# Roll layer of a fused two-block model: unread products gathered ahead of a step's first turns, the projection's bias moved to VectorE, and another split of the 32 images into groups

## The reference, cut to what matters

```python
h = h + _L1_attn_ref(_layernorm(h), W_A, W_V, W_O, b_O)
h = h + _L1_ffn_ref(_layernorm(h), ...)

def _L1_attn_ref(x, W_A, W_V, W_O, b_O):
    z = softmax(einsum('bse,he->bsh', x, W_A) * SCALING, axis=1)
    roll = z^T[:, :, (i - j) % S] * tril
    v = einsum('bse,fe->bsf', x, W_V)
    out = einsum('bhij,bjhd->bihd', roll, v)
    return einsum('bse,fe->bsf', out, W_O) + b_O
```

## Time and profile before

| | |
|---|---|
| median of 3 runs | 1064.62 us (1059.83 to 1065.32) |
| profiled execution | 1058.96 us, its span 1057.2 us |
| TensorE busy | 950.0 us (90%) |
| VectorE busy | 582.8 us (55%) |
| GpSimd busy | 519.2 us (49%) |
| ScalarE busy | 413.2 us (39%) |
| roll layer, first turn to last routing logits | 656.1 to 861.3 us of the span |

### The profile page before, as it was taken

The page is one execution under the profiler, slowest core; times in us unless marked ns, Lnnn a source line. Parts: engine busy times, 40 slices in busy tenths (PEclk is TensorE's granted clock), DMA queues, the critical chain, the costliest instruction groups (busy, mean ns, idle before and its releaser), DMA issues. The chain is left out here.

```text
span 1057.2 us, 29755 instructions
## 1 busy us (share of the span) xinstructions
PE 950.0 (90%) x10428; PEld 746.9 (71%) x10459; DVE 582.8 (55%) x1446; ACT 413.2 (39%) x1102; POOL 519.2 (49%) x714
## 2 busy tenths in 40 slices
PE   8899999998747999999999997689999957999996
PEld 6667777777634888888888875355556635888895
DVE  1778888865994777433333325677886452111111
ACT  2267677734243343343443422223333222332431
POOL 0055665620604777777777627777772002333432
PEclk9999999999969999999999998899999987999998
DMA  7010000002004988877788723334455047476750
GB/s 257 1 46 2 0 0 0 2 11 75 1 1 156 307 276 260 273 245 223 243 265 254 229 89 100 105 112 124 125 140 220 22 159 251 142 255 230 266 156 25
DMA packets 79821, 149.30 MB, mean 141 GB/s; under 512 B 18892, under 2 KB 53327, under 8 KB 75760
## 3 DMA queue, kind: packets, MB, share of 16 engines
q1 hardware_dynamic: 34768, 77.15, 21.5%
q0 software_dynamic: 17712, 47.88, 15.7%
q10 hardware_dynamic: 27248, 23.09, 6.5%
HBM read 200.22 MB, written 31.73 MB: 219 GB/s over the span
## 5 line engine op out<-in xcount | busy, mean ns | idle before, releaser
L1332 POOL DMA_INDIRECT x_x<-m_x_rows,x_idx x170 | 165.7, 975 | 74.7 <-issue 36.1
L1358 PE MATMUL x_pup<-x_xt,x_w 128*128 128x128 f32 (+1 forms) x2176 | 182.9, 250 | 0.0
L1358 PEld LDWEIGHTS x_pup<-x_xt,x_w 128*128 128x128 f32 (+1 forms) x2176 | 166.9, 165 | 5.9 <-issue 5.7
L1623 POOL DMA_INDIRECT rl_y<-m_y_rows,rl_idx x136 | 132.7, 976 | 43.6 <-issue 38.1
L1439 DVE TENSOR_TENSOR x_hid<-x_gate,x_pup 128x128 f32<-128x128 f32 x170 | 48.9, 287 | 147.9 <-ACT x_gate L1411 141.1
L1372 PE MATMUL x_pdown<-x_w,x_hid 128*128 128x256 f32 (+1 forms) x408 | 104.2, 389 | 0.2 <-DVE x_y L1446 0.2
L1407 ACT ACTIVATE x_xt<-x_pturn 128x256 f32<-128x256 f32 x170 | 65.2, 383 | 89.1 <-PE x_pturn L1343 86.4
L442 POOL TENSOR_TENSOR wa_probs<-wa_probs,wa_peak 68x544 f32<-68x544 f32 x64 | 69.9, 1092 | 57.6 <-DVE wa_peak L593 54.9
L2405 DVE TENSOR_TENSOR x_y<-x_pdown,x_b 128x256 f32<-128x256 f32 x21 | 8.9, 424 | 149.2 <-PE x_pdown L2359 149.2
L2391 ACT ACTIVATE x_hid<-x_pup,x_b 128x128 f32<-128x128 f32 (+1 forms) x200 | 52.6, 356 | 93.1 <-PE x_pup L2342 92.9
L1411 ACT ACTIVATE x_gate<-x_pup 128x128 f32<-128x128 f32 x170 | 47.1, 277 | 92.5 <-PE x_pup L1358 91.8
(11 more groups left out here) (345 smaller groups left out, 1917.9 us busy)
## 6 DMA issues: line engine op xcount, KB each, us to landing
x_w<-in_experts SPq DMA_DIRECT2D x204, 384.0 KB
late_w<-in_w SPq DMA_DIRECT2D x28, 1024.0 KB, 12.5
m_y_rows<-x_y ACTq DMA_DIRECT2D x170, 128.0 KB
xT<-in_w SPq DMA_DIRECT2D x12, 1024.0 KB, 7.0
xn<-in_w SPq DMA_DIRECT2D x10, 1024.0 KB, 11.5
h<-in_w SPq DMA_DIRECT2D x10, 1024.0 KB, 15.3
m_x_rows<-xn SPq DMA_DIRECT2D x34, 128.0 KB, 1.9
x_x<-m_x_rows,x_idx POOLq DMA_INDIRECT x170
```

Of the source, the lines that this page charges most:

```text
L1332: nc.gpsimd.indirect_dma_start(x[:, s, :], None, x_rows, bass.IndirectOffsetOnAxis(ap=idx[:, s:s + 1], axis=0))\
L1358: mm = nc.tensor.matmul(pup[rows:rows + wide, bank, m * P + side * wide:m * P + (side + 1) * wide], w[:, lane, first:first + wide], xt[:, ...
L1623: nc.gpsimd.indirect_dma_start(y[:, t % YR, kk, :], None, y_rows, bass.IndirectOffsetOnAxis(ap=idx[:, n:n + 1], axis=0))\
```

## The change

Four edits in `roll_layer`:

- Sizes: `[2] + [4] * 6 + [2] * 3`. There are now 10 groups and 13 steps; what was a group of 4 and one of 2 images at the end is now three groups of 2.
- Unread products: in steps where `1 < g1 < NG - 1` none stands between the parts any more, nor the wait that went with each. Six stand ahead of the first turn (three where the group has two images). In steps 1 and 2 there are 20 ahead of the first turn beside the old ones, in the last such step 4. After the last group the row of 8 is 5.
- Bias: `project` has no product with `b_o`. VectorE adds `b_o` to `h` with one instruction a tile, once the tile has been normalised.
- Loads of the guessed weights: ahead of group 4's stores. It was group 5 (`NG - 4` with `NG` = 9).

```diff
-    SIZES = [2] + [4] * 7 + [2]
+    SIZES = [2] + [4] * 6 + [2] * 3
...
-                    if g == NG - 4:
+                    if g == 4:
...
                     for s, t in enumerate(tiles_out(g)):
-                        nc.tensor.matmul(pr[:, s, :], ident, late["b_o"][:, :], start=True, stop=False)
                         for c in range(DC):
                             mm = nc.tensor.matmul(pr[:, s, :], aT[:, c, t * P:(t + 1) * P], late["w_o"][:, c, :],
-                                                  start=False, stop=(c == DC - 1))
+                                                  start=(c == 0), stop=(c == DC - 1))
                     mm.then_inc(projected, 1)
+
+                def steady(g):
+                    return 1 < g < NG - 1
...
                 def fill_values(g, n):
+                    if steady(g):
+                        return
                     pe.wait_ge(v_moved, pairs_through(g))
...
                 def fill_mid(g, n):
+                    if steady(g):
+                        return
...
+                    if has1:
+                        fill(g1, 6 * SIZES[g1] // GI if steady(g1) else 20 if g1 < 2 else 4)
                     for t in tiles_in(g1):
                         turn("in", t)
-                        fill(g1, 1)
+                        if not steady(g1):
+                            fill(g1, 1)
                     if has1:
-                        fill(g1, 1)
                         mix_logits(g1)
...
                     if has2 and not has1:
-                        fill(g2 + 1, 8)
+                        fill(g2 + 1, 5)
...
+                def add_out_bias(ts):
+                    for t in ts:
+                        dve.wait_ge(normed, turn_at["in", t] + 1)
+                        nc.vector.tensor_tensor(h[:, t, :], h[:, t, :], late["b_o"][:, :], ALU.add).then_inc(out_biased, 1)
+
                 def add_projected(g):
                     ts = tiles_out(g)
                     dve.wait_ge(projected, g + 1)
+                    dve.wait_ge(out_biased, ts[-1] + 1)
...
                     if outs:
                         scale("out", outs)
+                    add_out_bias(tiles_in(g1))
```

More of the change, by code:

```diff
@@ L1573, in roll_layer @@
         plog = po[:, GC:GC + NT * E1]
-        (indexed, set_up, added, in_measured, out_measured, logged, rooted, scaled, normed, turned, turn_moved, z_done, z_moved,
+        (indexed, set_up, added, out_biased, in_measured, out_measured, logged, rooted, scaled, normed, turned, turn_moved, z_done, z_moved,
          z_shifted, exped, z_normed, z_turned, zt_moved, zf_done, zf_moved, v_done, v_moved, forwarded, terms,
          inverted, out_moved, projected, proj_added, logits, rows_out, chain) = sems(
-            nc, k, "rl", "indexed set_up added in_measured out_measured logged rooted scaled normed turned turn_moved z_done "
+            nc, k, "rl", "indexed set_up added out_biased in_measured out_measured logged rooted scaled normed turned turn_moved z_done "
             "z_moved z_shifted exped z_normed z_turned zt_moved zf_done zf_moved v_done v_moved forwarded terms "
```

## The result

| | before | after |
|---|---|---|
| median | 1062.61 us (7 runs, 1058.72 to 1066.2) | 1072.28 us (7 runs, 1070.06 to 1081.79) |
| ratio, 95% interval | | 1.012 (1.0089 to 1.0151) |
| profiled execution | 1058.96 us, span 1057.2 | 1078.26 us, span 1076.5 |
| TensorE busy | 950.0 us (90%) | 959.8 us (89%) |
| VectorE busy | 582.8 us | 591.0 us |

The kernel became slower: by 9.7 us (0.9%) in the medians, and by 1.2% in the ratio over all runs, since the seven runs of after are spread upward. A gain was forecast. Its base was 1064.6 us, the median of three runs; seven runs put before at 1062.61.

The account below looks back on a forecast made before the run. TensorE bounds at 22.19 us a step, fetches close at 20.5. Last logits 7.6 us earlier (853.7), less 0.6 for the clock: gain 7.0, so 1064.6 becomes 1057.6 us; range 1052.5 to 1064.0.

Parts of the forecast that it names:

- Rival 3: TensorE idles some 3 us a step without products between parts, so the clock falls; 12 falls give 1072 us; chance 0.08.
- TensorE's step: Steps of 4 images: 2.91 us gained less 1.28 lost, so 20.56 us instead of 22.19, near the fetches' pace.
- Bias: VectorE's additions ahead of the combinations: 0.41 us each, 0.83 a step, covered by its wait for ScalarE.
- First steps: Turns at 656.1 to 696.40: fetches set them, and 20 products (4.3 us) fit into idle, nothing gained or lost.
- Loads: Moved to group 4, they delay tile 13's fetches by 3.3 us (0 to 7.4); its turn comes 2.4 us late.
- Clock behind that wait: Low clock behind the wait at 781 us, taken as half of 1.27 us: 0.6 us lost.
- Tail of small groups: From that turn to the last logits: 72.3 us instead of 76.3, 4.0 us less despite one step more.
- What follows keeps its length: Routing and experts behind the last logits take 196 us as before.

Follow-up runs that it names:

- e1: The changed kernel with the loads of guessed weights back ahead of group 5's stores: 1070.46 us, 1.0069 to before.
- e3: The changed kernel with loads back ahead of group 5 and the old unread products again in groups of 2 images: 1067.03 us, 1.0055 to before.
- e8: The changed kernel with the old sizes and the loads ahead of group 5; new product placing and bias stay: 1060.01 us, 0.9979 to before.
- e6: The kernel before with the bias on VectorE alone: 1057.25 us, 0.9945 to before.
- e7: The kernel before with the new placing of the unread products alone: 1074.41 us, 1.0115 to before.
- e2: The changed kernel, loads still at group 4, with the old unread products again in groups of 2 images: 1068.13 us, 1.0066 to before.
- f2: The changed kernel with six unread products put back in steady steps, four between the inversions and two behind: 1069.30 us, 1.0104 to before.
- f4: f1 less the four unread products around forward_mix in steady steps, 13 of 17 staying: 1050.59 us, 0.9922 to before.
- f1: The kernel before with the bias on VectorE and the loads ahead of group 6: 1057.59 us, 0.9967 to before.
- f3: The changed kernel with old sizes, loads ahead of group 6, six unread products moved from ahead of the turns to the inversions: 1052.86 us, 0.9927 to before.

## Why the prediction was wrong

It was wrong in direction: 1057.6 us forecast, 1072.28 measured, which is outside the range. Rival 3, the fall of the clock, is what happened; it had 0.08, and its price of 1072 is by accident the measured time: it is 12 falls of 1.27 us on a base 2 us too high, and the trace has fewer and longer ones. In the profiled execution the last logits were due at 853.7 us, ahead of the 0.6 for the clock, and came at 878.4. The 24.7 us, by the prediction's own steps:

- **TensorE's step, 20.56 us.** Right: 20.57 in after, e1, e3 and e8. So are its two parts, by e6 and e7, and so is the claim that fetches and VectorE keep up with it, since two steps followed each other at that length.
- **Bias, 0.41 us each and covered.** Right: 418 ns each, where the earlier trace rows has 415 for its neighbour, and nothing waited for it.
- **First steps, nothing lost by 20 products.** Wrong. They ran in part at the low clock and came last before the turn, which had no idle ahead of it:

```profile
673.16 6.32 PE L1712 MATMUL rl_pz<-m_chosen_b,m_before_b 128*128 128x512 bf16 x20
679.32 0.38 PE L1635 MATMUL rl_pt<-cst,xn 128*128 128x128 f32 x2
```

  I had taken 4.3 us for them, at the full clock. With a fall in the next step (0.85), the turn due at 717.2 came at 721.88; 1.25 of these 4.6 us is the later start of the layer.
- **Loads, tile 13 3.3 us late, within 0 to 7.4.** The mechanism was right, its size too small. The tile landed 6.0 us late against its issue (8.8 less 2.8). The way from landing to turn was as predicted, 782.06 + 6.28 = 788.34. The gather had been issued 4.2 us later than that of the earlier trace rows, partly because of the late start and the long first steps, so the cushion was 1.3 us. The turn was 4.7 us behind TensorE's own time, where 2.4 was forecast. Most of the missing packets are the first six us: 82 where 222 would be the pace of the earlier trace rows, and that deficit, 140 packets at 37 a us, is 3.8 us. The rest of the 6.0 is not explained. That the loads do it is shown by the other traces: TensorE idles 2.8 and 3.6 us ahead of this turn in e2 and f2, which have them at group 4, and not at all in e1 and e3. In medians the place of the loads is worth 1 to 2 us (e1 against after, e3 against e2), which is no more than the runs' spread.
- **Clock behind that wait, 0.6 us.** Mis-sized: the step took 24.86 us instead of 19.9, 5.0 us more.
- **Tail of small groups.** Predicted 16.1 and 11.9 us for the steps from 813.19 and 836.69, measured 23.50 and 16.84. The sums hold at the full clock: e3 takes 18.15 and 14.20, and these are 2.1 and 2.3 us above the predicted lengths, with some 15 old products more in each (0.215 us apiece, part of it in idle pieces). But without those products the clock was 0.65 and 0.70. 7.4 + 4.9 us are lost here, and 0.5 in the rest.
- **What follows keeps its length.** Nearly: 198.1 us instead of 195.9.

In the order of the program these are 4.6 + 2.3 + 5.0 + 7.4 + 4.9 + 0.5 = 24.7 us. The step that failed is a sentence in rival 3: "the fall in the trace came behind a whole stretch of idle of 2.75 us, none behind pieces below 1 us". It read the absence of falls in a step that had 17 products between its parts as if it told of a step without them. No row of this layer could show that case, so 0.08 had nothing behind it, and the range should have reached to the rival's price. In the sum it is the term for the clock, 0.6 us behind one wait and nothing elsewhere; in its place the executions of after spend some 30 us more at the lower level, at most 15 us of time, and the profiled one lost 5.0 + 7.4 + 4.9 us in three steps. I priced every unread product as time on TensorE and none as what it holds. The arithmetic of the rival was also off: it had one fall at 1.27 us, but a fall lasts for many pieces, and one step in e7 lost 26.09 - 21.43 = 4.7 us. What exactly between the bare products lets the clock fall, and why equal steps differ, stays open.

The Trainium skill (TensorE: Matmul & The Clock Gate, section on a second failure mode) tells of short, frequent idling that makes the clock go down and up, and was cited for this rival. e7's steps at 0.86, 0.80, 1.00 and 0.80, with idle pieces below 0.6 us, agree with the going down and up. That section ties it to a PSUM queue in bf16 products; no run here shows that.

## What to carry to other kernels

A product that nobody reads has two prices, the time it takes and the clock that it keeps, and the second shows in no trace in which it is still there; take such products out a few at a time and look at each step's granted clock. Here four of 17 could go with the clock at 1.00 in the trace (f4 against f1, 7.0 us in the medians). Eleven could go at no loss where the six that stayed stood at the inversions and all groups but the first and the last had four images (f3, 0.9927 against f4's 0.9922); with the six ahead of the turns it was between no gain (e8) and 1.2% slower (e7, after). When the durations of a plan turn out exact and the kernel is slower all the same, divide the length of one known instruction by that of the same instruction before (3.65 by 2.12 us): it finds the clock at once.

## What the runs showed of the hardware

- The clock fell in the middle of a step of float32 matmuls with no idle piece over 0.6 us ahead of it in that step (e7, 734.51 us). Equal steps of one execution took 21.43 and 26.09 us. Such falls began in the second of two inversions (64 products of 68x68 each) with nothing between them (e7, e8); with four bf16 products between them none began there (f2 and f3, nine steps).
- A fall can last far longer than the idle ahead of it: in after and e1 the steps of two images ran at 0.64 to 0.70 for 40 us, and in e3, with some 15 products more in each, at 1.00. The clock went up and fell anew several times without a longer wait (after: inversions of 2.12 us at 803.61 and 3.89 us at 823.59).
- 4 MB of plain loads put in front of running gathers delayed a gather by 6.0 us, with packets at 82 in six us, although the two queues are near even afterwards: 386 of the gathers and 402 of the loads in the next ten us of after.
